# GpSimd's batch of scales joins a pair's sums with the normed rows of the second last pair: one iteration of slack in the stage between two graph layers

## The reference, cut to what matters

```python
Y = X + Z                      # Z: sums over two steps, from the stage before
L0 = (Y - mu) / jnp.sqrt(var + 1e-5) * gamma + beta      # norm of the first layer
x = x + L0                                               # x1 in the kernel
h = jnp.maximum(_layernorm(x), 0.0)                      # h2 in the kernel
...
h_e = h @ edge_w;  support = h @ weight;  node = h @ node_w
```

## Time and profile before

| what | value |
|---|---|
| median of 3 runs | 3840.46 us |
| the profiled execution's own time | 3846.29 us |
| its span, first to last instruction | 3844.5 us |
| `phase_mid`, from its first load to its last VectorE instruction | 3145.99 to 3295.16 us |
| first VectorE instruction of `phase_edges` | 3297.89 us |
| granted TensorE clock, mean over the span | 0.888 |

### The profile page before, as it was taken

One profiled execution on the slowest core, in us unless ns is written; L12 is line 12 of the kernel. 1 busy time (PEld: TensorE's weight loads), 2 busy tenths in 40 slices (PEclk: granted clock), 3 DMA queues, 4 the chain that ended last, 5 costly groups with the idle time before them and its releaser, 6 DMA issues. The chain is left out here.

```text
span 3844.5 us, 41925 instructions
## 1 busy us (share of the span) xinstructions
PE 3004.2 (78%) x14148; PEld 2102.5 (55%) x14148; DVE 3540.4 (92%) x4636; ACT 3104.4 (81%) x4477; POOL 358.5 (9%) x417
## 2 busy tenths in 40 slices
PE   6568887787878776648978888796978536799999
PEld 4456666575656654414544545363544425577777
DVE  6999999999999999699999999999999969577776
ACT  6999999999999999399899999999999913233333
POOL 3000000000000000000000000000000017234443
PEclk9689889898988988869989999898989768899999
DMA  2112121222222220211111111111111025122221
GB/s 90 63 54 87 63 97 54 92 67 79 80 67 87 68 78 15 109 56 49 52 35 47 35 57 32 45 42 40 53 35 47 7 80 193 46 104 103 98 91 50
DMA packets 108904, 254.28 MB, mean 66 GB/s; under 512 B 11984, under 2 KB 47888, under 8 KB 105360
## 3 DMA queue, kind: packets, MB, share of 16 engines
q1 hardware_dynamic: 82768, 217.76, 17.6%
q10 hardware_dynamic: 25920, 33.83, 2.5%
HBM read 217.47 MB, written 34.08 MB: 65 GB/s over the span
## 5 line engine op out<-in xcount | busy, mean ns | idle before, releaser
L691 DVE SCALAR_TENSOR_TENSOR s_dump<-s_rows,s_mid 128x3327 bf16<-128x3327 f32 x608 | 2238.3, 3681 | 1.0 <-issue 0.6
L637 ACT ACTIVATE s_adump<-s_rows,s_mid 128x3327 int8<-128x3327 f32 x324 | 995.1, 3071 | 10.5
L643 ACT ACTIVATE s_adump<-s_rows,s_mid 128x3327 int8<-128x3327 f32 x324 | 990.8, 3058 | 0.0
L899 PE MATMUL bank<-x,s_slab 128*128 128x512 f32 x1352 | 629.3, 609 | 0.0
L876 PE MATMUL bank<-kh,qs 128*128 128x512 f16 (+1 forms) x364 | 146.4, 402 | 365.5 <-DVE s_rows L670 354.9
L899 PEld LDWEIGHTS bank<-x,s_slab 128*128 128x128 f32 x1352 | 265.4, 197 | 277.4 <-issue 265.6
L943 PE MATMUL bank<-hb,s_wT 128*128 128x256 f32 x1352 | 355.9, 408 | 70.7 <-ACT s_wT L515 70.7
L943 PE MATMUL bank<-xab,s_wT 128*128 128x256 f32 x1352 | 351.0, 405 | 71.8 <-ACT s_wT L515 71.6
L1334 ACT ACTIVATE e_wh<-bank 128x512 f16<-128x512 f32 (+1 forms) x182 | 102.4, 565 | 343.2 <-PE bank L1438 343.2
L932 PE MATMUL bank<-ident,s_rows 128*128 128x128 f32 x1352 | 229.7, 297 | 190.5 <-DVE s_rows L745 189.4
L899 PE MATMUL bank<-hb,s_slab 128*128 128x257 f32 x1352 | 358.1, 407 | 0.0
(11 more groups left out here) (176 smaller groups left out, 4806.1 us busy)
## 6 DMA issues: line engine op xcount, KB each, us to landing
s_slab<-adjT_dram SPq DMA_DIRECT2D x104, 448.0 KB, 3.9
e_adj<-adjR_dram SPq DMA_DIRECT2D x26, 1664.0 KB, 7.0
s_slab<-adjT_dram SPq DMA_DIRECT2D x104, 384.0 KB, 3.7
strip<-adjR_dram SPq DMA_DIRECT2D x52, 448.0 KB, 3.5
strip<-adjR_dram SPq DMA_DIRECT2D x52, 384.0 KB, 3.3
su_d<-s_su_out ACTq DMA_DIRECT2D x26, 256.0 KB, 2.0
zu_d<-s_zu_out ACTq DMA_DIRECT2D x26, 256.0 KB, 2.0
sx_d<-s_sx_out ACTq DMA_DIRECT2D x26, 256.0 KB, 2.0
```

The lines of the kernel that those rows point to most:

```text
L637: nc.scalar.activation(adump[:], row(g, r), ACT.Sign, bias=st(mid, g, 2), accum_out=cnt[:]).then_inc(S["a_eval"], 1)
L643: nc.scalar.activation(adump[:], row(g, r), ACT.Relu, bias=st(mid, g, 2), accum_out=gap[:]).then_inc(S["a_eval"], 1)
L691: nc.vector.scalar_tensor_tensor(out=dump[:], in0=row(g, r), scalar=st(mid, g, r), in1=row(g, r), op0=ALU.is_gt, op1=ALU.mult, accum_out=s ...
L899: ins = nc.tensor.matmul(acc, slab[:, i % NSLAB, j - PIECES[p], :], s_op[:, j, 0:SN], start=False, stop=(j == NT - 1))
```

## The change

Batch i now joins the sums of pair i with the normed rows of pair i - 2. VectorE writes the moments of the normed rows of pair i - 1 into the cell of batch i + 1, and the batch's wait goes from 4i + 2 increments of `moments` to 4i, which is reached by the moments of the sums in iteration i. `positive` of pair q takes its scales from batch q + 2, and the last two pairs both from batch 13 (there is no batch 14; the last pair's moments go to the two free places of that batch's cell). `low_parts` follow their pair by four iterations, not three, so VectorE's loop has one iteration more at the end.

```diff
-    LAG = 3
+    LAG = 4
...
             def inverse_roots(i):
                 k = i % CELLS
-                pool.wait_ge(S["moments"], 4 * i + 2 if i < NPAIR else 4 * NPAIR)
-                if i >= CELLS:
-                    pool.wait_ge(S["h2_ready"], 2 * (i - CELLS))
+                pool.wait_ge(S["moments"], max(2, 4 * i))
+                if i >= CELLS + 2:
+                    pool.wait_ge(S["h2_ready"], 2 * (i - CELLS - 1))
...
-            def moments(i, w):
+            def moments(i, w, v):
                 for k in range(2):
-                    nc.vector.bn_aggr(mv[:, i % CELLS, w + k], stat[:, w + k]).then_inc(S["moments"], 1)
+                    nc.vector.bn_aggr(mv[:, i % CELLS, w + k], stat[:, v + k]).then_inc(S["moments"], 1)
...
                     statistics(x1, 2 * (i - 1) % 6, 2)
-                    moments(i, 2)
+                    if i < NPAIR:
+                        moments(i + 1, 2, 2)
+                    else:
+                        moments(i, 0, 2)
...
             def positive(t):
                 i, k = divmod(t, 2)
-                cell = (i + 1) % CELLS
-                act.wait_ge(S["roots_ready"], i + 2)
+                batch = min(i + 2, NPAIR)
+                cell, w = batch % CELLS, 0 if i == NPAIR - 1 else 2
+                act.wait_ge(S["roots_ready"], batch + 1)
```

More of the change, by code:

```diff
@@ L1176, in _ @@
                     statistics(y, 2 * i % 4, 0)
-                    moments(i, 0)
+                    moments(i, 0, 0)
                 if i >= LAG:
@@ L1194, in positive @@
                 i, k = divmod(t, 2)
-                cell = (i + 1) % CELLS
-                act.wait_ge(S["roots_ready"], i + 2)
+                batch = min(i + 2, NPAIR)
+                cell, w = batch % CELLS, 0 if i == NPAIR - 1 else 2
+                act.wait_ge(S["roots_ready"], batch + 1)
                 if t >= 4:
                     act.wait_ge(S["ht_done"], t - 3)
-                nc.scalar.activation(h2[:, t % 4], x1[:, t % 6], ACT.Relu, scale=inv[:, cell, 2 + k:3 + k],
-                                     bias=nmr[:, cell, 2 + k:3 + k]).then_inc(S["h2_ready"], 1)
+                nc.scalar.activation(h2[:, t % 4], x1[:, t % 6], ACT.Relu, scale=inv[:, cell, w + k:w + k + 1],
+                                     bias=nmr[:, cell, w + k:w + k + 1]).then_inc(S["h2_ready"], 1)
             def columns(t):
```

## The result

The changed kernel takes 3837.78 us, the median of 20 runs (3834.09 to 3840.03); the kernel before takes 3842.08 us in 20 runs on the same chips (3840.18 to 3844.36). The sign was right and the size a third of what was forecast.

A forecast was written before the change was run, and what follows sets the result against it. The prediction took a closed loop of waits between GpSimd's batch and VectorE, 9.40 us a period, to bound the stage. Loop gain 16.5, less 0.5 at the end and 1.3 on loads, gave 14.7 us: 3825.8 us, range 3821 to 3835.

The forecast's parts named there:

- The closed loop and what opens it: GpSimd and VectorE wait for each other each 9.40 us; batch i, waiting only for first moments, opens this toward 7.58.
- the early intervals: Iterations 2 to 4, without low parts: GpSimd sets the pace, two intervals between first moments at 7.9 us.
- Nothing is added or removed; every duration above stays: All instruction times read before the change were taken to hold after it, the batch at 4.49 us among them.
- GpSimd's bare cycle: Batch 4.49 us plus side sums of 0.68 each, 7.2 in all, 0.4 faster than VectorE's bare iteration of 7.58.
- Ten intervals: From first moments of iteration 2 to those of iteration 12: 94.0 us before, 77.5 after, a gain of 16.5.
- Side sums on add_up or short of it: Forecast: side sums stop short of add_up; rival 1: they land on it, 7.5 us less gained, 3833, chance 0.2.
- the lock: Port pair shared by VectorE and GpSimd is held per instruction: late side sums wait, VectorE loses nothing, gain stays 16.5.
- The end: From first moments of iteration 12 to the stage's end: 29.8 us before, 30.3 after, a loss of 0.5.
- TensorE's clock (rivals 2 and 3): Pairs bound the stage: at 8.1 us, 3831, chance 0.17; at 9.3, 3846, chance 0.06 with other ways to lose.
- Loads: Tile loads have less slack where the next stage's 1664 KB loads stand between, three places: 1.3 us lost in all.
- Sum: Whole stage: 16.5 - 0.5 - 1.3 = 14.7 us gained, passed on whole to the kernel's time.

The follow-up runs named there:

- narrow add_up: Changed kernel with add_up working on 4 of 256 columns from tile 4 on: 3828.79 us, ratio 0.9965.
- short side sums: Changed kernel with beta added to 4 of 256 columns, which shortens two of the four side sums of a pair: 3827.22 us, ratio 0.9963.
- one round: One round of Newton's steps on GpSimd, not two: 3829.19 us on the changed kernel, 3827.52 us on the kernel before.
- the experiment on the last normalize: Changed kernel with iteration 13's low parts moved behind the last pair's normalize and statistics: 3835.60 us, ratio 0.9983.
- LAG = 4: Kernel before with LAG = 4 and not 3, the batches wired as before: 3841.72 us, ratio 1.0001.

## Why the prediction was wrong, by its own steps

**The closed loop and what opens it: right.** GpSimd's waits for the moments fell from 26.9 to 6.2 us. How far it opens was wrong from the start: the early intervals, forecast at 7.9, are 8.35: the batch took 4.95 there and not 4.5.

**"Nothing is added or removed; every duration above stays": this is the step that failed.** The batch of 4.49 us was read where add_up lay beside its one long instruction. Moved by the new wait, it lies elsewhere: the long instruction beside normalize's end and the statistics, four of the small ones beside add_up, each 0.12 to 0.24 longer. The sign was in the prediction's own rows: batch 13, with no add_up about, takes 4.2 and not 4.49. I had GpSimd's bare cycle at 7.2, 0.4 below VectorE's 7.58; it is 5.2 + 2.7 = 7.9, and with the gap ahead of the batch 8.0, above VectorE's. So GpSimd does not gain on VectorE, the side sums stay on normalize, and being slowed there they add another 0.5. Ten intervals took 84.3 us (3171.2 to 3255.5) where I had 77.5: a gain of 9.7, not 16.5. That accounts for 6.8 us of the miss. The narrow add_up, with the batch at 4.22 us and no instruction of GpSimd touched, shows what made the batch longer. That the loop would have run at 7.6 with a batch of 4.49 is not shown: in the two kernels where only GpSimd's work was cut, it ran at 7.0 to 7.8 with one interval of 8.2 (short side sums), which is the pace forecast, but at 7.5 to 8.7 with the shorter batch (one round). I had taken the slowing as VectorE's loss alone, and looked for it on wide GpSimd instructions only.

**Side sums on add_up or short of it.** In the changed kernel the question did not arise. Where it did, in the changed kernel with one round, they did run into add_up, at 7.5 to 8.7 us a pair. The Trainium skill's page "SBUF — State Buffer", section "SBUF: two separate sides", gives an exclusive lock on a port pair that both engines share, the loser blocked for the whole instruction. The traces agree as far as they go: a small GpSimd instruction of 0.20 takes up to 0.44 beside one of VectorE of 0.48, and ends 0.05 to 0.06 us after it, as if waiting it out. But from the lock I had argued that a late side sum meets the last instruction of add_up, waits, and costs VectorE nothing. In the one-round kernel it first comes at 3190.72, beside the third instruction, and takes 0.92 us; the fourth begins at 3191.09 and takes 0.83 and not 0.48. A cycle later the side sums are on the first two. So the waiting went both ways, and the rule of the lock left open what I took from it.

**The end: right in kind, too small.** Forecast 30.3, measured 31.6 and 29.95. But I set it against 29.8, which was the long end of a single profile; a second profile has 26.1. Between the means of the two profiles of each kernel the loss is 2.9 us and not 0.5. Term by term, the terms of the forecast first: from the first moments of iteration 12 to batch 13, 9.1 and measured 11.2 in both profiles; batch 13, 4.2 and 4.2; pair 11, 9.3 and 8.4 or 6.8; pair 12 and its last low part, 7.7 and 7.7. The term that was missed is pair 9. Its low parts come late and hold VectorE up for 2.0 us ahead of the last normalize, because what is left of iteration 12 and iteration 13 are short, about 4.5 us each. Pair 11's better time hid a part of this.

Behind that stands a cost of the wiring itself. A pair now waits for the second batch behind its own and not the first, so one pair more is left when VectorE comes to its end. At the first moments of iteration 12 the next pair to begin is pair 9, where it was pair 10. With the stall taken out (the experiment on the last normalize) four pairs of 6.8 us follow each other, and the end is 28.4 us. With the old wiring three are left, and the end was 26.1, 25.6 with LAG = 4, and 22.2 with one round. That this is the whole of the difference is argued, not shown.

**TensorE's clock (rivals 2 and 3): not the limit.** Pairs, from `positive` to the last high part, alternate between about 6.8 and 8.4 us at a period of 8.42; the granted clock in the stretch of the earlier trace rows is 0.83 against 0.80. VectorE does not wait for low parts in mid stage.

**Loads (1.3 us): as good as nothing in this kernel.** GpSimd waited 0.6 us for a load in the stage. In the kernel with one round it waited 3.9 us between 3190 and 3250, so the slack was as thin as worked out.

**Sum.** By the means of two profiles each, the loop gave 9.7 us, the end took 2.9 and the way to iteration 2 took 0.4, which is 6.5 for the stage (150.3 against 143.8 us); the medians show 4.3 and 4.8. The 2 us between are not explained. The profiled executions of one kernel differ by 3.5 to 4.4 us, and the first one of before, at 3846.3, lies above all 20 runs (3844.4 at most), so the profiles may make the gain look larger than it is.

## What to carry to other kernels

A wait that is removed moves the work behind it to another place beside the other engine, and durations read in the old place need not hold there: before adding them up, lay the new schedule beside the other engine's and price each overlap, also for instructions that are tiny. Two engines that slow each other can settle where their cycles are equal (8.42 and 8.41 us here), without any wait between them in the trace; then look for rows of one kind with different durations, not for idle time. A result that is taken one batch later shortens the wait in the loop and leaves one piece of work more behind it at the end: price both. And price the end of a pipelined stage from more than one profile: one pair there at a granted clock of 0.64 instead of 1.00 cost 2.2 us, half of the whole gain.

## What the runs showed of the hardware that I had not expected

VectorE's two-input instructions on 128 x 256 make 128 x 4 instructions on GpSimd slow: 0.20 us becomes 0.32 to 0.44, four beside four, and it is 0.20 again when the VectorE instructions shrink to four columns. VectorE's own four stay at 0.45 to 0.48 beside them. The power instruction takes 1.04 beside nothing of that kind and up to 1.24 beside it. Taking 1.1 us from GpSimd's batch gave 14.6 us in the kernel before, three times the change under study, though GpSimd was not busy all the time there: the batch is a link of the closed loop, and with it the side sums moved.
